# Causal mask of an attention: from a matrix product on TensorE to the VectorE instruction that finds the row maximum

## The reference, cut to what matters

```python
x = L0_attn_x
x = x + 0.5 * ffn(layernorm(x), ...)
x = x + attn(layernorm(x), w_q, w_k, w_v)
x = x + 0.5 * ffn(layernorm(x), ...)

def attn(x, w_q, w_k, w_v):          # m = 1024, d = 128
    q_rot, k_rot = rotate(x @ w_q.T), rotate(x @ w_k.T)     # rotary embedding
    v = x @ w_v.T
    scores = q_rot @ k_rot.T / sqrt(d)
    scores = where(tril(ones((m, m))), scores, -inf)
    return softmax(scores) @ v
```

## Time and profile before

| | before |
|---|---|
| median of 3 runs | 911.74 us (911.11 to 914.44) |
| the profiled execution | 913.98 us, span 912.1 us |
| PE, DVE, ACT, POOL busy | 96%, 82%, 64%, 54% of the span |
| attention stage | about 366 to 589 us of the span |
| one sequence in its middle | 27.95 us |

### The profile page before, as it was taken

One profiled execution on the slowest core, in us unless ns is written; L12 is line 12 of the kernel. 1 busy time (PEld: TensorE's weight loads), 2 busy tenths in 40 slices (PEclk: granted clock), 3 DMA queues, 4 the chain that ended last, 5 costly groups with the idle time before them and its releaser, 6 DMA issues.

```text
span 912.1 us, 18507 instructions
## 1 busy us (share of the span) xinstructions
PE 872.8 (96%) x4608; PEld 730.3 (80%) x4608; DVE 748.7 (82%) x2245; ACT 582.7 (64%) x1189; POOL 491.5 (54%) x476
## 2 busy tenths in 40 slices
PE   4799999999999996999999999999999999999997
PEld 3688888888888875899988898878888888888885
DVE  4688888888888887888898888588888888888884
ACT  5476666666666754666666666766666666666664
POOL 4466666666666665222232232066666666666665
PEclk9999999999999997899999999999999999999999
DMA  8745444455534440000000000164445555444662
GB/s 264 222 113 131 106 93 93 95 119 129 124 94 93 94 94 0 1 2 1 1 0 0 0 0 1 46 142 108 105 106 123 137 136 127 105 105 106 132 140 65
DMA packets 52590, 81.06 MB, mean 89 GB/s; under 512 B 5328, under 2 KB 17488, under 8 KB 52304
## 3 DMA queue, kind: packets, MB, share of 16 engines
q1 hardware_dynamic: 52560, 80.71, 37.3%
HBM read 75.45 MB, written 5.24 MB: 88 GB/s over the span
## 4 chain that ended last, share of the span: by engine, by line
PE 50%; DVE 4%; issue 4%; ACT 3%; POOL 1%; DMA 1%; DVEq 0%; ACTq 0%; SPq 0%; POOLq 0%
PE bank L1030 43%; PE bank L1222 3%; PE bank L1182 2%; DVE rot L876 1%; PE bank L1063 1%; PE bank L1042 1%; PE bank L1171 1%; ACT prob L548 1%; ACT qkv_both L425 1%; DVE qkT L897 1%; DVE rope_c L888 1%; DMA qkT<-comb_rows 0%; DVE negmax L905 0%; DVE xn L634 0%; ACT probT L425 0%
## 5 line engine op out<-in xcount | busy, mean ns | idle before, releaser
L340 POOL TENSOR_TENSOR h_l<-probT,h_h 128x512 fp32r<-128x512 f32 x256 | 330.6, 1292 | 224.1 <-ACT h_h L425 224.0
L1030 PE MATMUL bank<-xh,w_h 128*128 128x512 f32 x544 | 225.6, 415 | 5.2 <-DVE prob L720 5.1
L720 DVE TENSOR_TENSOR prob<-bank,qkT 128x512 f32<-128x512 f32 x256 | 176.1, 688 | 65.3 <-ACT bank L454 40.8
L425 ACT ACTIVATE h_h<-probT 128x512 fp32r<-128x512 f32 (+1 forms) x288 | 180.3, 626 | 75.0 <-DVE probT L728 73.7
L454 ACT ACTIVATE bank<-bank 128x512 f32<-128x512 f32 x256 | 148.7, 581 | 116.3 <-PE bank L1030 111.4
L1030 PE MATMUL bank<-xh,w_l 128*128 128x512 f32 x544 | 217.1, 399 | 0.0
L1030 PE MATMUL bank<-xl,w_h 128*128 128x512 f32 x544 | 217.0, 399 | 0.0
L728 DVE TENSOR_TENSOR probT<-prob,bank 128x512 f32<-128x512 f32 x256 | 174.4, 681 | 10.8 <-DVE biased L669 5.2
L1030 PEld LDWEIGHTS bank<-xh,w_h 128*128 128x128 f32 x544 | 103.7, 191 | 28.2 <-issue 5.4
L1030 PEld LDWEIGHTS bank<-xh,w_l 128*128 128x128 f32 x544 | 103.4, 190 | 25.0
L1030 PEld LDWEIGHTS bank<-xl,w_h 128*128 128x128 f32 x544 | 103.8, 191 | 19.9
(11 more groups left out here) (93 smaller groups left out, 1340.2 us busy)
## 6 DMA issues: line engine op xcount, KB each, us to landing
qkT<-comb_rows SPq DMA_DIRECT2D x256, 256.0 KB, 5.5
out_x<-X SPq DMA_DIRECT2D x16, 256.0 KB, 6.5
comb_rows<-combT SPq DMA_DIRECT2D x32, 32.0 KB, 1.8
cos<-in_cos SPq DMA_DIRECT2D x1, 1024.0 KB, 8.9
sin<-in_sin SPq DMA_DIRECT2D x1, 1024.0 KB, 10.9
qkv_both<-in_w13T SPq DMA_DIRECT2D x1, 832.0 KB, 5.4
qkv_both<-in_w2T SPq DMA_DIRECT2D x1, 576.0 KB, 7.7
X<-in_x SPq DMA_DIRECT2D x1, 512.0 KB, 6.6
```

Of the source, the lines that this page charges most:

```text
L340: nc.gpsimd.tensor_tensor(lo, f, hi.bitcast(F32), ALU.subtract).then_inc(done, 1)
L425: return nc.scalar.activation(dst, src, ACT.Copy)
L720: nc.vector.tensor_tensor(weighted[j % 2], bank[:, G_BANK[(q + j) % 2], :], comb_b[q][:, j, :], ALU.mult).then_inc(weighted_done, 1)
L1030: return nc.tensor.matmul(dst, lhsT, rhs, start=start, stop=stop)
```

## The change

The mask is no longer a product on PE. DVE's instruction for the maximum becomes `tensor_tensor_reduce`: it reads the scores in PSUM and a mask in SBUF, writes -(scores + mask) back over the scores, and gives the minimum of what it wrote, which is minus the row maximum. ACT's exponential reads with a scale of -1.0. The mask is now 128 x 1152 float32, zeros ahead of the triangle, so that a slice of it covers all (i + 1) x 128 columns; it is loaded straight to its tile, and ACT's two rounding copies and PE's wait for them are gone. On DVE the reciprocal of step i now stands in front of the maximum of step i + 1, with its wait for the exponential of step i and behind the wait for the scores of i + 1; `attn_max` itself waits for nothing.

```diff
-        mask = sb("mask", [P, P], F32R)
-        ident_r = sb("ident_r", [P, P], F32R)
+        mask = sb("mask", [P, M + P])
...
-                    load(mask_f, mask_d, attn_loaded)
+                    load(mask[:], mask_d, attn_loaded)
...
-                    copy(mask[:], mask_f).then_inc(consts_rounded, 1)
-                    copy(ident_r[:], ident[:]).then_inc(consts_rounded, 1)
...
-                                     ACT.Exp, bias=negmax[s][:],
+                                     ACT.Exp, bias=negmax[s][:], scale=-1.0,
...
             def attn_max(b, i):
                 s, w = i % 2, (i + 1) * P
-                wait(dve, exp_done, QB * b + i - 1)
-                dve.wait_ge(scores_ready, QB * b + i + 1)
-                nc.vector.reduce_max(negmax[s][:], bank[:, 2 * s:2 * s + 2, :].rearrange("p a c -> p (a c)")[:, 0:w],
-                                     AX_X, negate=True).then_inc(negmax_done, 1)
+                row = bank[:, 2 * s:2 * s + 2, :].rearrange("p a c -> p (a c)")[:, 0:w]
+                nc.vector.tensor_tensor_reduce(row, row, mask[:, M - i * P:M + P], -1.0, 0.0 - MASKED, ALU.add, ALU.min,
+                                               negmax[s][:]).then_inc(negmax_done, 1)
...
                 for i in range(QB):
                     if i == 5 and not last:
                         attn_stats(b + 2)
+                    if i + 1 < QB or not last:
+                        dve.wait_ge(scores_ready, QB * b + i + 2)
+                    attn_rrow(b, p, i)
                     if i + 1 < QB:
                         attn_max(b, i + 1)
...
-                    attn_rrow(b, p, i)
...
-                    diag = c == i // 4
-                    ins = mm3(dst, qkT_h[p][:, 0, qs], qkT_l[p][:, 0, qs], qkT_h[p][:, 1, k0:k1], qkT_l[p][:, 1, k0:k1],
-                              True, not diag)
-                    if diag:
-                        ins = mm(bank[:, 2 * s + c, k1 - k0 - P:k1 - k0], ident_r[:], mask[:], False, True)
+                    ins = mm3(dst, qkT_h[p][:, 0, qs], qkT_l[p][:, 0, qs], qkT_h[p][:, 1, k0:k1], qkT_l[p][:, 1, k0:k1])
```

More of the change, by code:

```diff
@@ L169, in macaron @@
         parts, at = {}, 0
-        for name, blocks in (("w13", 2 * UNITS - 1), ("w2", UNITS), ("wqkv", 3), ("mask", 1)):
+        for name, blocks in (("w13", 2 * UNITS - 1), ("w2", UNITS), ("wqkv", 3)):
             parts[name] = staged[:, at:at + blocks, :]
@@ L173, in macaron @@
         w13_f, w2_f = parts["w13"], parts["w2"]
-        wqkv_f, mask_f = (parts[n].rearrange("p n c -> p (n c)") for n in ("wqkv", "mask"))
+        wqkv_f = parts["wqkv"].rearrange("p n c -> p (n c)")
         x_loaded = [sem(f"x_loaded{n}") for n in range(3)]
@@ L186, in macaron @@
         wqkv_hi = sem("wqkv_hi")
-        consts_rounded = sem("consts_rounded")
         gw_split = sem("gw_split")
@@ L1014, in _ @@
                 attn_item(item, 0, 0, True)
+            dve.wait_ge(scores_ready, 1)
             attn_max(0, 0)
@@ L1138, in ffn @@
                     pe.wait_ge(wqkv_split, 1)
-                    pe.wait_ge(consts_rounded, 2)
                 ffn_tile(T, 1, False, True, False, start)
@@ L1324 @@
     mask = np.where(col > row, np.float32(MASKED), np.float32(0.0)).astype(np.float32)
+    mask = np.concatenate([np.zeros((P, M), np.float32), mask], axis=1)
     cos, sin = rope_tables()
```

## The result

The changed kernel has a median of 916.28 us (914.24 to 916.85, 11 runs), the kernel before 912.22 us (910.43 to 914.44, 11 runs, taken alongside); the ratio is 1.004, with a 95% interval of [1.003, 1.005]. It is 4.1 us slower. The forecast was 910.9 with a range to 915.0: the sign was wrong, and the time lies outside the range.

What follows compares the result with a forecast made beforehand. PE was taken to pace some 18 of each attention sequence's 28 us, DVE the rest. Middle sequences -1.0 us, last +0.1, start 0: about -0.9 us, 910.9 us on the 911.74 median; range 908.5 to 915.0.

Steps and rivals of the forecast that it cites:

- The mask product: Removing it from PE in the attention: 0.06 us each, 0.11 behind narrow scores; 0.35 us saved a sequence.
- the PE-bound part: Some 18 of a sequence's 28 us, paced by PE; only the five mask products there count, three others give nothing.
- The main part of the new instruction: DVE's masked maximum in the attention, without its accumulator output: taken as unchanged, about 0.68 us over 512 columns.
- Rival 1: DVE becomes the bound, new instruction at half rate: 2.5 to 3 us a sequence, 931 us; 7% for slower by over 0.5%.
- The accumulator read: Writing out the minimum on DVE: 0.07 us a maximum, bounds 0 and 0.20; two maxima count in the DVE-bound part.
- five further maxima: Maxima in the PE-paced part of a sequence: 0.35 us more on DVE, covered by its gaps.
- The order on DVE: Reciprocal ahead of the next maximum: the link through ACT's copy to DVE's split 0.07 us longer in a middle sequence.
- The last sequence: Later maxima in the attention's end: 0.3 us charged, 0.1 of it at `xn`, less some 0.2 for masks: +0.1.
- rival 3: The tail or the start slips: late maxima 0.5 and 0.4 us, start 0.7; +1.5 us, 912.4; 13%.
- rival 4: The granted clock, lower at the attention's beginning, could move by a us or two either way; 5%, within the range.
- The milder form of rival 1: A fixed surcharge of 0.2 to 0.4 us for each DVE maximum: 914 to 917 us; 10%.
- the sum for a middle sequence: +0.21 us in the DVE-bound part, -0.35 in the PE-bound part: net -0.14, seven times, -1.0 us.

Runs made afterwards that it cites:

- run 7: Kernel before with the 64 mask products on PE left out and nothing in their place (attention not causal); 909.61 us, ratio 0.9979.
- run 5: Changed kernel with DVE's attention loop written out and DVE's old order and waits restored; 911.72 us, ratio 0.9993; once more 911.81 us, 1.0005.
- run 6: Kernel before with the reciprocal ahead of the maximum and the changed kernel's waits, mask products and plain maximum kept; 913.29 us, ratio 1.0023.
- run 1: Changed kernel with DVE's attention loop (three turns of two sequences) written out; 912.03 us, ratio 0.9999.
- experiment 4: Changed kernel, waits ahead of DVE's loop moving it 32 instructions: 913.17 us, or 128: 921.6 us; kernel before with smaller pad in the loop: 912.62 us; single executions.

## Why the prediction was wrong, point by point

"Run" with a number is the experiment of that number.

- *The mask product.* Right. 0.35 us a sequence was forecast, 0.34 measured (run 7). The reading that only the PE-bound part counts holds: all eight would have been 0.53.
- *The main part of the new instruction.* Right: 0.67 us over 512 columns, at the rate of the maximum. Rival 1 falls. (Its price was mis-summed besides: 4608 columns less 896 are 3712, not 3840, and its own terms, 0.9 and 3.9 less 1.1, come to 3.7 us a sequence, not 2.5 to 3.)
- *The accumulator read.* Right in the sum, not in the place. 0.07 us a maximum was charged to DVE's queue, twice in the chain, 0.14 a sequence. The rows show no time on the queue from 384 columns on, and 0.06 us until ACT has the maximum. Run 5 has all but the order of the change; against run 7, which has only PE's part, its exponentials over 384, 512 and 640 columns start 0.06, 0.12 and 0.18 us later after the start of the sequence, and a sequence is 0.07 or 0.20 us longer, 0.14 on the mean. So three maxima pay on the way, where two were counted. The 0.35 us more on DVE for five further maxima don't exist either; the sum had called them covered, so this does no harm.
- *The order on DVE.* Mis-sized: 0.07 us forecast, 0.2 measured (run 5) or 0.15 (run 6). Between run 1 and run 5, ACT's exponential over 384 columns starts 0.07 us later after the start of the sequence, that over 512 columns 0.13, that over 640 columns 0.20. That fits one reciprocal in front of each maximum for which ACT waits, adding up along the chain; the prediction counted one of three.
- *The last sequence.* Mis-sized: +0.3 us (less 0.2 for masks) forecast, 0.7 to 0.8 measured, in runs 1 and 6 too. The late `xn` showed 0.4 us where 0.1 was charged: the exponential over 384 columns, which was taken for its cover, came later itself, 3.81 us behind that of block 0 in place of 3.48.
- *Rivals 3 and 4.* The last sequence did slip, by 0.8 us, as rival 3 has it, but that alone is no 4 us. The granted clock is 1.00 in the sequences shown, long ones too, so rival 4 is not what lengthens them. At the start of the attention it may play a part: from 370 to 374 us the granted clock is 0.63 in the profile before and 1.00 in that after, whose attention also begins earlier. The milder form of rival 1 has the time right (914 to 917) and the cause wrong: the read costs 0.06 us, not 0.2 to 0.4.
- *The step that failed:* the sum for a middle sequence, "Net -0.14 us, seven times", took the sequences for equal. Two of them begin with a branch back of DVE's loop, and the change put 20 instructions into its body. The branches then cost 3.3 and 3.5 us of DVE's sequencer, and those two sequences end 1.4 and 1.6 us later than before. The term was put at nothing without a reason: the sum has none for the loop. No rival had it, though the Trainium skill's section named in experiment 4 warns of such stops; I hadn't weighed it against the loop's length. It was shown from both sides: taken away by writing the loop out and by moving it 32 instructions, brought back by moving it 128 (these two in one execution each), and made in the kernel before by a pad without engine work. Shown is that the loop's length and place bring the stops, together with packets on the instruction queue; that the sequencer waits for these packets is the reading of both.

The account of a middle sequence: -0.34 us for PE, +0.14 for the read, +0.2 for the order, about nothing, where -0.14 was forecast; with the loop written out the six sequences take 167.2 us, exactly as before. The account of the kernel, against the kernel before: 2.6 us for the two stops, 0.7 for the first sequences of the loop's three turns, which in the changed kernel are 0.25 us longer each even without a stop (28.16 us in run 4 against 27.91 in run 1), and 0.8 for the last sequence.

What stays open: what takes the 0.25 us in the first sequence of a turn, whether the change moves the start of the attention, and the 1.4 us that run 5 lost at its end, twice. Of the last, part is the clock. Of run 5, then of run 1, PE's last transposes and the granted clock (the 1.00, 0.84 or 0.50 in the busy windows' rows; 0.50 is the lower of its two levels, 1.2 GHz):

```profile
904.60 1.07 PE L1060 MATMUL bank<-ident,probT 128*128 128x128 f32 x4 [0.69 <-ACT probT L423]
```

```profile
904.00:905.00 1.00, 0.40 (x2) 0.40 (x3) 0.00 (x0) 0.55 (x1) 0.00 (x0) 0.84 0.00 0
905.00:906.00 1.00, 0.67 (x4) 0.27 (x2) 0.29 (x1) 0.00 (x0) 0.00 (x0) 0.50 0.00 0
```

```profile
905.18 0.66 PE L1061 MATMUL bank<-ident,probT 128*128 128x128 f32 x4 [0.69 <-ACT probT L423]
```

```profile
905.00:906.00 1.00, 0.66 (x4) 0.42 (x4) 0.12 (x1) 0.13 (x1) 0.00 (x0) 1.00 0.00 0
```

From 902 to 903 and from 903 to 904 us, ahead of the fall, PE was busy for 0.79 and 0.73 us in run 5, more than in run 1 (0.60 and 0.62), so it isn't a longer pause of PE that explains the fall. The rest is the last store, which landed 3.3 us after its issue in place of 2.3 (3.1 the second time). Why both come with this kernel wasn't tried.

## What to carry to other kernels

Adding instructions to a loop has a price of its own that no row of the kernel before shows: where a loop's body of 277 or 280 instructions lay badly, each branch back stopped DVE's sequencer for over 3 us. Look at the packets of the instruction queue and at idle time put down to "issue" right behind a branch, and write the loop out before judging a change by its time. When work moves from a full engine to one that others wait for, count each wait along the chain, not one in a sequence: 0.07 us in front of three of them was 0.2 us. And ask of a second instruction's row who pays for it, the queue or the engine that waits.

## What the runs showed of the hardware that wasn't expected

- A branch back on DVE took 0.27 to 0.30 us with bodies of 260, 264 and, at one place, 280 instructions, and 3.2 to 3.7 us with bodies of 277 and, at two places, 280; packets on the instruction queue rose from 17 or 18 to 28 or 29. The loops of the feed-forward, with bodies of 213 and 214, never showed it (0.27 to 0.37 us).
- The custom DVE instruction with two streams, a write back to PSUM and a running minimum runs at the maximum's own rate: 0.28 us over 128 columns and 1.22 over 1024. Its result comes by a second instruction, 0.14 us in its row, which held DVE's queue for nothing behind 384 columns and more and gave ACT the result 0.06 us later.
- 256 waits that were already met, in 128 instructions with two waits each, held DVE for 12.7 us, 0.1 us an instruction.
